# One attention and feed-forward layer: the closing output projection moved into the main block, with f16 operands

## The chip, the core and the metric

The kernel runs on one core of a Trainium2 chip. The core has five engines with instruction streams of their own: TensorE (PE, matrix products), VectorE (DVE), ScalarE (ACT), GpSimd (POOL) and SyncE (SP, which here only issues DMAs). They share the on-chip memory SBUF. Products land in PSUM, eight banks of 128 x 512 f32. Engines wait for one another by semaphores. The metric is the device time of one execution in microseconds; lower is better.

## What is computed

For x of 2048 tokens by 512 features, with xn the layer norm of x:

```
out  = x + attention(xn) @ Wo + bo + ffn(xn)
attention: 16 heads of 32, 4 key/value heads, causal, ALiBi bias
ffn: (gelu(xn @ Wg.T) * (xn @ Wu.T)) @ Wd.T, 4096 wide; Wg, Wu, Wd are unpacked from 4-bit codes and scales
```

The kernel keeps f32 accuracy by splitting operands into a rounded high part and a low part and adding three products (high x high, high x low, low x high).

## The kernel before

`preamble` normalises x, projects q, k and v into DRAM (`q_parts`, `k_parts`, `v_parts`) and computes scales, among them `oscale`, a scale for each output column that the `down` sums lack.

`main_loop` is a second block: 16 bodies, one for each attention head and, beside it, one sixteenth of the feed-forward width. A body has 48 slots, written out by hand in tables; every engine walks the same slots in program order. In a slot TensorE computes one block of scores (`score`, L1140, into the single bank `score_ps`), one or two products for the row maxima (`maximum`, L1118, into the two banks `pair_ps`, that is `max_ps` and `turn_ps`, in turn), half a piece of `gate` or `up` or a `down` tile (`mlp`, L1106 and L1086), and at some slots a batch of `values` (L1149). ScalarE turns a block of scores into exponentials (L1238), then into f16 (`phi`, L1245). TensorE's next score waits until the exponential has read the bank. GpSimd takes the low parts (`plo`, L1415). VectorE reduces maxima (L1342, L1338), adds `down` tiles to `acc` (`accumulate`, L1289), does the gelu products and, from slot 26 on, decodes the next weights (`decode_step`); TensorE turns these (L345), and ScalarE and VectorE copy them to `wh` (L352) and `wl` (L357).

A head's output leaves by another way (`output_steps`): ScalarE copies it out of PSUM (L1257, L1260), SyncE gathers it in SBUF (`gather_o`, three parts) and sends the row sums to `l_parts` in DRAM. In the next body SyncE loads the sums (`load_sums`), VectorE adds and inverts them (`row_sums`, slot 14), SyncE stores and spreads the reciprocals (`store_recips`, `spread_recips`), and GpSimd adds the parts (slots 19 and 23) and multiplies (`normalise`, slot 36). SyncE stores the result as f32 in `o_heads`.

`epilogue` is a third block. Every engine enters it after SyncE has left the second. It loads Wo, all heads' outputs and x, brings the last head through the same steps, splits Wo and the outputs into high and low parts (L1508, L1514, L1522), multiplies (`project`, L1531), turns `oscale` into a row by a product with ones, multiplies `acc` by it (L1587), adds x and the bias (L1591, L1566), adds the product (L1596) and stores 16 tiles.

## Time and profile before

| what | value |
|---|---|
| median of 3 runs | 1768.53 us (1766.18 to 1768.92) |
| profiled execution, own time | 1768.29 us |
| its span, first to last instruction | 1766.5 us |
| TensorE busy | 1677.6 us (95%) |
| VectorE, ScalarE, GpSimd busy | 1339.7, 1074.1, 963.7 us |

The profile lists, for one execution, when each instruction ran and what an engine waited for before it (in square brackets: the idle time, and who ended it). The numbers below count from the span's start. A timeline merges neighbours of the same kind (x4). The chain of waits is followed back from the last instruction to whatever released each step.

### The profile page before, as it was taken

How to read it: one execution, taken by the hardware profiler on the slowest of the kernel's cores; microseconds unless marked ns; L12 is line 12 of the kernel's file. 1: busy time of each engine (PE TensorE's matmuls, PEld its weight loads, DVE VectorE, ACT ScalarE, POOL GpSimd, SP SyncE). 2: the span in 40 equal slices, each digit the busy share in tenths (PEclk: the TensorE clock that was granted, in tenths of full speed). 3: DMA queues.
4: the chain of work that ended last, by engine and by line, in shares of the span. 5: the costliest groups of instructions: out<-in, count | busy, mean ns of one | idle time of the engine just before them, and what ended most of it. 6: DMA issues, size and time to landing. Idle time of an engine off the chain costs nothing. (4 is left out here: it accounts for less than half of the span.)

```text
span 1766.5 us, 30945 instructions
## 1 busy us (share of the span) xinstructions
PE 1677.6 (95%) x10368; PEld 854.4 (48%) x10368; DVE 1339.7 (76%) x2785; ACT 1074.1 (61%) x1779; POOL 963.7 (55%) x801
## 2 busy tenths in 40 slices
PE   4989999999999999999999999999999999999957
PEld 3764444444444444444444444444444444444435
DVE  6767778777777777787777777777777777777739
ACT  2336757575756667575857576766758575757610
POOL 3306647374655556473746565664737464656617
PEclk9999999999999999999999999999999999999979
DMA  6770020212020211202020202012030212020154
GB/s 192 201 192 18 20 69 17 74 26 75 26 69 18 70 29 30 70 17 76 24 74 27 70 21 78 16 42 59 17 81 20 74 26 74 21 73 17 46 176 155
DMA packets 94825, 109.49 MB, mean 62 GB/s; under 512 B 39068, under 2 KB 58524, under 8 KB 92876
## 3 DMA queue, kind: packets, MB, share of 16 engines
q1 hardware_dynamic: 94668, 107.53, 22.4%
q8 instruction: 83, 1.36, 0.3%
q14 instruction: 74, 0.61, 0.1%
HBM read 72.22 MB, written 22.41 MB: 54 GB/s over the span
## 5 line engine op out<-in xcount | busy, mean ns | idle before, releaser
L1415 POOL TENSOR_TENSOR plo<-p,phi 128x512 f16<-128x512 f32 (+1 forms) x576 | 669.8, 1174 | 317.8 <-ACT phi L1245 316.1
L1238 ACT ACTIVATE p<-score_ps,pshift 128x512 f32<-128x512 f32 (+1 forms) x576 | 382.2, 663 | 284.3 <-DVE score_ps L1327 155.7
L1245 ACT ACTIVATE phi<-p 128x512 f16<-128x512 f32 (+1 forms) x576 | 350.0, 608 | 15.3
L1423 POOL TENSOR_TENSOR il<-prod,ih 128x512 f16<-128x512 f32 x128 | 160.9, 1257 | 335.5 <-DVE ih L1321 335.5
L1140 PE MATMUL score_ps<-qst,kst 128*128 128x512 f32 (+3 forms) x640 | 305.6, 494 | 13.0 <-ACT p L1238 11.4
L1289 DVE TENSOR_TENSOR acc<-down_ps,acc 128x512 f32<-128x512 f32 x253 | 172.7, 682 | 70.0 <-PE down_ps L1086 70.0
L1342 DVE TENSOR_REDUCE mxp<-max_ps 128x1 f32<-128x512 f32 x256 | 175.5, 686 | 53.5 <-PE max_ps L1118 53.5
L1106 PE MATMUL gate_ps<-xh,wh 128*128 128x512 f16 x512 | 198.7, 388 | 0.0
L1106 PE MATMUL up_ps<-xh,wh 128*128 128x512 f16 x512 | 198.0, 387 | 0.0
L1086 PE MATMUL down_ps<-wh,ih 128*128 128x512 f16 x506 | 195.9, 387 | 0.9 <-DVE acc L1289 0.9
L1106 PE MATMUL gate_ps<-xh,wl 128*128 128x512 f16 x512 | 194.8, 380 | 0.0
L1106 PE MATMUL gate_ps<-xl,wh 128*128 128x512 f16 x512 | 194.7, 380 | 0.0
L1106 PE MATMUL up_ps<-xh,wl 128*128 128x512 f16 x512 | 194.0, 379 | 0.0
L1106 PE MATMUL up_ps<-xl,wh 128*128 128x512 f16 x512 | 194.0, 379 | 0.0
L1086 PE MATMUL down_ps<-wl,ih 128*128 128x512 f16 x506 | 191.8, 379 | 0.0
L1086 PE MATMUL down_ps<-wh,il 128*128 128x512 f16 x506 | 191.8, 379 | 0.0
L1140 PEld LDWEIGHTS score_ps<-qst,kst 128*128 128x128 f32 x640 | 116.3, 189 | 111.5 <-ACT p L1238 48.4
L1149 PE MATMUL o_ps<-phi,vst 128*32 128x512 f16 (+3 forms) x1744 | 164.4, 348 | 0.0
L1118 PE MATMUL max_ps<-kst,qst 128*128 128x512 f32 (+2 forms) x320 | 151.4, 473 | 10.3 <-SPq L1007 4.8
L1118 PE MATMUL turn_ps<-kst,qst 128*128 128x512 f32 (+3 forms) x320 | 141.2, 441 | 1.6 <-DVE mxp L1338 1.6
L1149 PE MATMUL o_ps<-plo,vst 128*32 128x512 f16 (+3 forms) x1024 | 136.2, 342 | 0.0
L1222 ACT ACTIVATE gl<-gate_ps,cur 128x512 f32<-128x512 f32 x128 | 87.8, 686 | 67.9 <-issue 42.6
(201 smaller groups left out, 2919.2 us busy)
## 6 DMA issues: line engine op xcount, KB each, us to landing
qst<-q_parts SPq DMA_DIRECT2D x204, 64.0 KB
kst<-k_parts SPq DMA_DIRECT2D x48, 256.0 KB, 6.1
o<-oraw SPq DMA_DIRECT2D x192, 64.0 KB
vst<-v_parts SPq DMA_DIRECT2D x16, 512.0 KB, 5.9
q_parts<-o SPq DMA_DIRECT2D x24, 256.0 KB, 3.3
raw<-L_ffn_gate_W_packed_dram SPq DMA_DIRECT2D x18, 256.0 KB, 2.8
raw<-n_L_ffn_up_W_packed_dram SPq DMA_DIRECT2D x18, 256.0 KB, 3.2
raw<-L_ffn_down_W_packed_dram SPq DMA_DIRECT2D x18, 256.0 KB, 3.9
```

What stands on the lines that cost most here:

```text
L1086: mm = nc.tensor.matmul(dst[:], lhs, rhs, start=(q == 0), stop=(q == 5))
L1106: mm = nc.tensor.matmul(dst[:], lhs, rhs, start=(q == 0), stop=(q == 11))
L1118: mm = nc.tensor.matmul(dst[:, 0:cols], qst[:, c, t * P:(t + 1) * P], kst[par][:, m * CH:m * CH + cols], start=True, stop=True)
L1140: mm = nc.tensor.matmul(score_ps[:, col:col + width], kst[par][:, j * P:(j + 1) * P], qst[:, c, tok:CH], start=True, stop=True, skip_group ...
L1149: mm = nc.tensor.matmul(bank[g * HD:(g + 1) * HD, tok:CH], vst[:, j, of * HD:(of + 1) * HD], src[n % PP][:, col:col + CH - tok], start=sta ...
L1222: nc.scalar.activation(gl[a][:], gate_ps[:], ACT.Square, scale=cur[par][:, a:a + 1]).then_inc(square_done, 1)
L1238: nc.scalar.activation(p32[n % PR][:, 0:cols], score_ps[:, 0:cols], ACT.Exp, bias=pshift[:, 0:1]).then_inc(exp_done, 1)
L1245: nc.scalar.activation(phi[n % PP][:, 0:cols], p32[n % PR][:, 0:cols], ACT.Copy).then_inc(phi_done, 1)
L1289: nc.vector.tensor_tensor(acc[:, n % NT, :], bank[:], acc[:, n % NT, :], ALU.add).then_inc(acc_done, 1)
L1342: nc.vector.tensor_reduce(mxp[c % 2][:, t, m:m + 1], pair_ps[n % 2][:, 0:cols], AX.X, ALU.max).then_inc(red_done, 1)
L1415: nc.gpsimd.tensor_tensor(plo[n % PP][:, 0:cols], p32[n % PR][:, 0:cols], phi[n % PP][:, 0:cols], ALU.subtract).then_inc(plo_done, 1)
L1423: nc.gpsimd.tensor_tensor(il[w % 2][:, a, :], prod[a][:], ih[w % 2][:, a, :], ALU.subtract).then_inc(il_done, 1)
```

## The change

The third block is gone; its work stands at the end of the second block's programs.

- Outputs of heads are stored as two f16 halves: `output_hi` on ScalarE at slot 38 and `output_lo` on GpSimd at slot 39 of the next body. The copies out of PSUM lose their scale operand; the scale goes into `yback`.
- Column scales and their inverses are turned into rows in the preamble (a transposition of 8 rows, a copy, a DMA). The `down` sums start from the bias times the inverse (`bias_row`), so `acc` is no longer cleared. VectorE, no longer GpSimd, writes the four constants at the start of the block.
- In the last body nothing is decoded or loaded for a next head. Wo is loaded at its start; VectorE looks for its largest element at slots 17 to 20 (eight reductions), scales at slot 29, and ScalarE and VectorE make its f16 halves at slots 31 to 35. The outputs of earlier heads are loaded for the first two of four blocks of 512 tokens.
- Behind the loop TensorE does the first three of four groups for eight tiles before, between and behind the last `down` tiles; the last group, which holds the last head, follows. ScalarE issues part of the loads, the bulk ones of blocks 2 and 3 late.
- In `gather_o` the row sums go first, in two DMAs and not four, with semaphores of their own; the reciprocals are spread by one DMA and not four.

```
-ADD_PARTS_AT, NORMALISE_AT = (19, 23), 36
+ADD_PARTS_AT, NORMALISE_AT, BIAS_AT = (19, 23), 36, 11
+OUTPUT_HI_AT, OUTPUT_LO_AT = 38, 39
+WO_MAX_AT, WO_SCALE_AT, WO_HI_AT = (17, 18, 19, 20), 29, (31, 32, 33, 34)
...
+        nc.gpsimd.tensor_tensor(o[:, 0, :], o[:, 0, :], o[:, step + 1, :], ALU.add).then_inc(osum_done, 1)
...
+    def output_hi(act, h):
+        act.wait_ge(on_done, h + 1)
+        if h:
+            act.wait_ge(on_out, 32 * h)
+        nc.scalar.activation(onh[:], o3[h % 2][:, 0, :], ACT.Copy).then_inc(ohi_done, 1)
+
+    def output_lo(pool, h):
+        pool.wait_ge(ohi_done, h + 1)
+        if h:
+            pool.wait_ge(on_out, 32 * h)
+        nc.gpsimd.tensor_tensor(onl[:], o3[h % 2][:, 0, :], onh[:], ALU.subtract).then_inc(olo_done, 1)
...
+                        pe.wait_ge(os_done, 1)
+                        pe.wait_ge(xl_done, KT * NCH)
+                        nc.tensor.transpose(turn[0][0:2 * KT, 0:P], oboth, ident[:]).then_inc(os_turned, 1)
...
                     load_v(i)
-                    load_k(nxt, 1 - par)
+                    if i < LAST:
+                        load_k(nxt, 1 - par)
+                    else:
+                        load_early()
+                    if i == 0:
+                        sp.wait_ge(os_out, 16)
+                        for row, src in ((column_inv, os_s[1]), (bias, bo)):
...
+                        if i == LAST and c == NCH - 2:
+                            spread_tops()
+                        if i == LAST and c == NCH - 1:
+                            sp.wait_ge(wo_lo, KVH)
+                            load_x(sp, 0)
...
-                    for m in range(3):
-                        sp.wait_ge(wf_done, (i + 1) * 6 + 2 * m + 2)
-                        load_raw(sp, m, (i + 2) % HEADS)
+                    if i + 2 < HEADS:
+                        for m in range(3):
+                            sp.wait_ge(wf_done, (i + 1) * 6 + 2 * m + 2)
+                            load_raw(sp, m, i + 2)
...
                 def gather_o(i, c, par):
                     sp.wait_ge(oraw_done, after(2 * (i * NCH + c + 1)))
                     if c == 0 and i >= 2:
-                        sp.wait_ge(on_done, i - 1)
+                        sp.wait_ge(ohi_done, i - 1)
+                        sp.wait_ge(olo_done, i - 1)
+                    if c == 0 and i == 1:
+                        sp.wait_ge(acc_done, after(NT))
+                    cols = slice(c * CH, (c + 1) * CH)
+                    sp.dma_start(l_s[par, 0:1, cols], oraw[c % 2][VPARTS * HD:VPARTS * HD + 1, :]
+                                 ).then_inc(l_out[c % 2], 16)
+                    sp.dma_start(l_s[par, 1:LPARTS, cols], lraw[0:(LPARTS - 1) * HD:HD, :]
+                                 ).then_inc(l_out[c % 2], 16)
                     for part in range(VPARTS):
                         sp.dma_start(o3[par][c * HD:(c + 1) * HD, part, :],
                                      oraw[c % 2][part * HD:(part + 1) * HD, :]).then_inc(o_out[c % 2], 16)
-                    cols = slice(c * CH, (c + 1) * CH)
-                    sp.dma_start(l_s[par, 0:1, cols], oraw[c % 2][VPARTS * HD:VPARTS * HD + 1, :]
-                                 ).then_inc(o_out[c % 2], 16)
-                    for q in range(1, LPARTS):
...
+                def load_early():
+
+                    sp.wait_ge(wf_done, 6 * HEADS)
+                    sp.wait_ge(wturn_done, 6 * HEADS)
+                    for g in range(KVH):
+                        sp.dma_start(wo[g], Wo.rearrange("(r g d) n -> g r d n", r=REP, g=KVH)[g]).then_inc(wo_in, 16)
...
+                    sp.wait_ge(on_out, 32 * (HEADS - REP))
+                    load_full(sp, 0)
...
+                    sp.wait_ge(wtop_done, 1)
+                    sp.dma_start(w_s.rearrange("(p o) -> p o", o=1), wtop).then_inc(wtop_out, 16)
+                    sp.wait_ge(wtop_out, 16)
+                    sp.dma_start(wall, w_s.rearrange("(o n) -> o n", o=1).broadcast_to([P, P])).then_inc(wall_in, 16)
+                    sp.wait_ge(down_done, after(LAST * ND))
+                    load_full(sp, 1)
...
+                load_sums(sp, LAST)
+                store_recips(sp, LAST)
+                spread_recips(sp, LAST)
+                sp.wait_ge(olo_done, HEADS)
+                load_last(sp, 1, onl)
+                for n in range(NT):
+                    sp.wait_ge(y_read, n + 1)
+                    sp.dma_start(out_d[n * P:(n + 1) * P, :], acc[:, n, :]).then_inc(out_done, 16)
...
-                        if s in TURN_W_AT:
+                        if s in TURN_W_AT and i < LAST:
...
+                def project(n, groups):
+
+                    c, t = n // TPC, n % TPC
+                    for g in groups:
+                        for q, (part, rhs) in enumerate(((0, woh), (0, wol), (1, woh))):
+                            mm = nc.tensor.matmul(y_ps[n % len(y_ps)][:], out_part(part, c, g)[:, t * P:(t + 1) * P],
+                                                  rhs[:, g, :], start=(g == 0 and q == 0), stop=(g == KVH - 1 and q == 2))
+                    if KVH - 1 in groups:
+                        mm.then_inc(y_done, 1)
+
                 loop(pe, body)
+                first, last = range(KVH - 1), range(KVH - 1, KVH)
+                pe.wait_ge(wo_lo, KVH)
+                pe.wait_ge(o_in[0], 16 * FULL_DMAS[0])
+                pe.wait_ge(red_done, after(HEADS * NMAX))
+                for n in range(2):
+                    project(n, first)
                 pe.wait_ge(gelu_done, after(HEADS * GU))
                 pe.wait_ge(prod_done, after(HEADS * GU))
                 pe.wait_ge(exp_done, after(HEADS * NBLK))
                 for t in range(TPC):
                     for half in range(2):
                         down(HEADS * NCH - 1, t, half, (down_ps, gate_ps, up_ps, score_ps)[t])
+                pe.wait_ge(oraw_done, after(2 * HEADS * NCH))
+                for n in range(2, TPC):
+                    project(n, first)
+                pe.wait_ge(o_in[1], 16 * FULL_DMAS[1])
+                for t in range(TPC):
+                    pe.wait_ge(acc_done, after((HEADS * NCH - 1) * TPC + t + 1))
+                    project(TPC + t, first)
+                for n in range(NT):
+                    if n % TPC == 0:
+                        pe.wait_ge(o_in[n // TPC], 16 * (FULL_DMAS[n // TPC] + 2))
+                        pe.wait_ge(last_in[n // TPC], 32)
+                    if n >= len(y_ps):
+                        pe.wait_ge(y_read, n - len(y_ps) + 1)
+                    project(n, last if n < len(y_ps) else range(KVH))
 
             @block.scalar
             def _(act):
@@ -1253,10 +1410,11 @@
                         done = BATCH_OF[BLK_END[c] - 1] + 1
...
                 loop(act, body)
+                act.wait_ge(on_out, 32 * LAST)
+                for c in range(2):
+                    load_rest(act, c)
+                act.wait_ge(il_done, after(HEADS * GU))
+                load_x(act, 1)
+                act.wait_ge(up_done, HEADS * GU)
+                load_full(act, 2)
+                load_rest(act, 2)
+                output_hi(act, LAST)
+                act.wait_ge(ohi_done, HEADS)
+                load_last(act, 0, onh)
+                load_full(act, 3)
+                load_rest(act, 3)
+                for c in range(2, NCH):
+                    load_x(act, c)
 
...
-                    nc.vector.tensor_tensor(acc[:, n % NT, :], bank[:], acc[:, n % NT, :], ALU.add).then_inc(acc_done, 1)
+                    before = acc[:, n % NT, :] if n >= NT else bias_row
+                    nc.vector.tensor_tensor(acc[:, n % NT, :], bank[:], before, ALU.add).then_inc(acc_done, 1)
...
+                        if i == LAST and s in WO_MAX_AT:
+                            wo_max(WO_MAX_AT.index(s))
+                        if i == LAST and s == WO_SCALE_AT:
+                            wo_scale()
+                        if i == LAST and s - 1 in WO_HI_AT:
+                            wo_low(WO_HI_AT.index(s - 1))
+                        if i == LAST:
+                            continue
...
+                    nc.vector.tensor_reduce(wmost[:, g:g + 1], wo[g], AX.X, ALU.max).then_inc(wmax_done, 1)
+                    nc.vector.tensor_reduce(wleast[:, g:g + 1], wo[g], AX.X, ALU.min).then_inc(wmax_done, 1)
...
+                def scale_sums(c):
+                    part = acc[:, c * TPC:(c + 1) * TPC, :]
+                    dve.wait_ge(acc_done, after((HEADS - 1) * NT + (c + 1) * TPC))
+                    if c == 0:
+                        dve.wait_ge(column_in, 16)
+                    nc.vector.tensor_tensor(part, part, column.unsqueeze(1).broadcast_to([P, TPC, C]), ALU.mult
+                                            ).then_inc(scaled, 1)
+
+                def add_x(c):
+                    dve.wait_ge(scaled, c + 1)
+                    dve.wait_ge(x_back[c], 16 * len(xr[c]))
+                    tiles = TPC // len(xr[c])
+                    for k, x in enumerate(xr[c]):
+                        part = acc[:, c * TPC + k * tiles:c * TPC + (k + 1) * tiles, :]
+                        last = nc.vector.tensor_tensor(part, part, x, ALU.add)
+                    last.then_inc(base_done, 1)
+
+                nc.vector.memset(pshift[:], PSHIFT).then_inc(pshift_done, 1)
+                nc.vector.memset(mask_row[:, 0:CH - P], 0.0).then_inc(mask_done, 1)
+                nc.vector.tensor_copy(mask_row[:, CH - P:], mask_ts[:]).then_inc(mask_done, 1)
+                nc.vector.tensor_scalar(identr[:], ident[:], 1.0, 1.0, ALU.mult, ALU.mult).then_inc(identr_done, 1)
                 dve.wait_ge(mask_done, 2)
                 loop(dve, body)
+                scale_sums(0)
...
                 loop(dve, body)
+                scale_sums(0)
+                add_x(0)
                 for t in range(TPC):
+                    if t == 2:
+                        row_sums(dve, LAST)
                     accumulate((HEADS * NCH - 1) * TPC + t, (down_ps, gate_ps, up_ps, score_ps)[t])
+                for c in range(1, NCH):
+                    scale_sums(c)
+                add_x(1)
+                for n in range(NT):
+                    if n >= 2 * TPC and n % TPC == 0:
+                        add_x(n // TPC)
+                    dve.wait_ge(y_done, n + 1)
+                    dve.wait_ge(base_done, n // TPC + 1)
+                    nc.vector.scalar_tensor_tensor(acc[:, n, :], y_ps[n % len(y_ps)][:], yback, acc[:, n, :],
+                                                   ALU.mult, ALU.add).then_inc(y_read, 1)
...
-                nc.gpsimd.memset(mask_row[:, 0:CH - P], 0.0).then_inc(mask_done, 1)
-                nc.gpsimd.tensor_copy(mask_row[:, CH - P:], mask_ts[:]).then_inc(mask_done, 1)
-                nc.gpsimd.tensor_scalar(identr[:], ident[:], 1.0, 1.0, ALU.mult, ALU.mult).then_inc(identr_done, 1)
-                nc.gpsimd.memset(pshift[:], PSHIFT).then_inc(pshift_done, 1)
-
-                nc.gpsimd.memset(acc[:], 0.0).then_inc(acc_done, 1)
...
+                        if i == 0 and s == BIAS_AT:
+                            pool.wait_ge(bias_in, 32)
+                            nc.gpsimd.tensor_tensor(bias_row, bias, column_inv, ALU.mult).then_inc(acc_done, 1)
...
+                        if i and s == OUTPUT_LO_AT:
+                            output_lo(pool, i - 1)
```

How the instructions stand, at three places. First TensorE, at the end of the loop. Before, the last half tile of the loop (`ih0`, `il0`) is followed by the last `down` tiles:

```order
L1086 MATMUL down_ps<-wh1,ih0 128x512
L1086 MATMUL down_ps<-wl1,ih0 128x512
L1086 MATMUL down_ps<-wh1,il0 128x512
L1086 MATMUL down_ps<-wh1,ih1 128x512
L1086 MATMUL down_ps<-wl1,ih1 128x512
L1086 MATMUL down_ps<-wh1,il1 128x512
```

Now (`turn_ps` and `max_ps` are output banks 0 and 1, `kst0` holds loaded outputs, `wl0` and `wh0` the high and low half of Wo):

```order
L1213 MATMUL down_ps<-wh1,ih0 128x512
L1213 MATMUL down_ps<-wl1,ih0 128x512
L1213 MATMUL down_ps<-wh1,il0 128x512
L1337 MATMUL turn_ps<-wl0,kst0 128x512
L1337 MATMUL turn_ps<-wh0,kst0 128x512
L1337 MATMUL turn_ps<-wl0,kst0 128x512 x2
```

Eighteen products with Wo, nine for each bank, stand ahead of the `down` tiles. Second, ScalarE in slots 38 and 39 of a body, before:

```order
L1238 ACTIVATE p32_2<-score_ps,pshift 128x512
L352 ACTIVATE wh1<-turn_ps 128x512
L1245 ACTIVATE phi5<-p32_2 128x512
L1228 ACTIVATE gl0<-gl0,cur0 128x512
L1238 ACTIVATE p32_0<-score_ps,pshift 128x512
```

Now (`o3_1` holds the last head's output, `onh` its f16 half):

```order
L1395 ACTIVATE p32_2<-score_ps,pshift 128x512
L285 ACTIVATE onh<-o3_1 128x512
L354 ACTIVATE wh1<-turn_ps 128x512
L1402 ACTIVATE phi5<-p32_2 128x512
L1385 ACTIVATE gl0<-gl0,cur0 128x512
L1395 ACTIVATE p32_0<-score_ps,pshift 128x512
```

The copy stands between the exponential of slot 38 and the weights' copy. Third, VectorE in slots 17 and 18 of the last body, before:

```order
L1321 CAST ih1<-prod0 128x512
L1342 TENSOR_REDUCE mxp1<-max_ps 128x1
L1289 TENSOR_TENSOR acc<-down_ps,acc 128x512
L1342 TENSOR_REDUCE mxp1<-turn_ps 128x1
L1342 TENSOR_REDUCE mxp1<-max_ps 128x1
```

Now (`wf` holds half of Wo, `sc0` the extremes found):

```order
L1505 CAST ih1<-prod0 128x512
L1526 TENSOR_REDUCE mxp1<-max_ps 128x1
L1592 TENSOR_REDUCE sc0<-wf 128x1
L1593 TENSOR_REDUCE sc0<-wf 128x1
L1473 TENSOR_TENSOR acc<-down_ps,acc 128x512
L1526 TENSOR_REDUCE mxp1<-turn_ps 128x1
L1592 TENSOR_REDUCE sc0<-wf 128x1
L1593 TENSOR_REDUCE sc0<-wf 128x1
L1526 TENSOR_REDUCE mxp1<-max_ps 128x1
```

Two reductions stand behind the maximum in front of the accumulation, and two behind the next one.

## Rows read from the trace of the kernel before

**Rows 1.** Waits chain that ended last: start us, duration us, what.
```profile
1688.89 11.29 DMA lp<-l_parts
...
1700.78 2.56 DMA l_recips<-lrec
...
1704.65 1.99 DMA rb<-l_recips
```
**Rows 2.** Windows: stretch, length, busy us (count) by engine, clock, DMA, GB/s.
```profile
160.00:1574.00 1414.00, 1400.21 (x8935) 677.23 (x8935) 1094.67 (x2318) 938.93 (x1558) 814.93 (x690) 1.00 0.17 45
...
1682.00:1766.50 84.50, 52.47 (x200) 41.57 (x200) 51.20 (x37) 9.77 (x6) 39.62 (x9) 0.81 0.51 168
```
**Rows 3.** Timeline of TensorE, slots 45 to 47: start us, us, instruction.
```profile
1669.33 0.38 PE L1106 MATMUL up_ps<-xh,wh 128*128 128x512 f16 x1
...
1671.70 0.38 PE L1106 MATMUL up_ps<-xl,wh 128*128 128x512 f16 x1
...
1675.05 0.38 PE L1086 MATMUL down_ps<-wh,il 128*128 128x512 f16 x1
```
**Rows 4.** Timeline of TensorE, closing block, its first idle stretch.
```profile
1726.79 0.50 PE L1531 MATMUL y_ps<-woh,och 128*128 128x512 f32 x1 [2.13 <-DVE xr L1596]
...
1728.16 0.63 PE L1531 MATMUL y_ps<-woh,ocl 128*128 128x512 f32 x1
1728.58 0.63 PE L1531 MATMUL y_ps<-woh,och 128*128 128x512 f32 x1
```
**Rows 5.** Timeline of VectorE, closing block.
```profile
1714.88 2.29 DVE L1587 TENSOR_TENSOR acc<-acc,orow 128x2048 f32<-128x2048 f32 x1
...
1732.62 6.52 DVE L1591 TENSOR_TENSOR acc<-acc,xr 128x2048 f32<-128x2048 f32 x1
...
1761.32 2.49 DVE L1596 TENSOR_TENSOR xr<-y_ps,acc 128x512 f32<-128x512 f32 x4
```
**Rows 6.** Timeline of GpSimd, closing block.
```profile
1730.40 6.59 POOL L1508 TENSOR_TENSOR ocl<-xl,och 128x2048 fp32r<-128x2048 f32 x1
```
**Rows 7.** Timeline of SyncE, last head's gather.
```profile
1675.93 2.94 SPq L1042 DMA_DIRECT2D o<-oraw  x3
```
**Rows 8.** Timeline of ScalarE, head 15, slots 38 and 39.
```profile
1654.84 0.70 ACT L1238 ACTIVATE p<-score_ps,pshift 128x512 f32<-128x512 f32 x1
...
1655.89 0.66 ACT L1245 ACTIVATE phi<-p 128x512 f16<-128x512 f32 x1
1656.41 0.75 ACT L1228 ACTIVATE gl<-gl,cur 128x512 f32<-128x512 f32 x1
1657.03 0.71 ACT L1238 ACTIVATE p<-score_ps,pshift 128x512 f32<-128x512 f32 x1
```
**Rows 9.** Timeline of TensorE, head 15, slot 40.
```profile
1657.79 0.49 PE L1140 MATMUL score_ps<-qst,kst 128*128 128x512 f32 x1 [0.30 <-ACT p L1238]
```
**Rows 10.** Waits of TensorE, 300:1575: total us, times, longest.
```profile
PE score_ps L1140 <- ACT p L1238: 8.5, 28, 0.3
```
**Rows 11.** Timeline of GpSimd, head 15, slot 36.
```profile
1653.98 1.46 POOL L279 TENSOR_TENSOR on<-on,rb 128x512 f32<-128x512 f32 x1
```
**Rows 12.** Timeline of VectorE, head 15, slots 19 to 21.
```profile
1617.91 0.69 DVE L1342 TENSOR_REDUCE mxp<-max_ps 128x1 f32<-128x512 f32 x1 [0.64 <-PE max_ps L1118]
...
1621.28 0.69 DVE L1289 TENSOR_TENSOR acc<-down_ps,acc 128x512 f32<-128x512 f32 x1 [2.08 <-PE down_ps L1086]
```
**Rows 13.** Timeline of TensorE, head 15, one turn of weights and what follows.
```profile
1665.34 0.60 PE L345 MATMUL turn_ps<-ident,wf 128*128 128x128 f32 x4
1665.69 0.48 PE L1140 MATMUL score_ps<-qst,kst 128*128 128x384 f32 x2
```
**Rows 14.** Timeline of ScalarE, then TensorE, start of the main block.
```profile
130.46 0.69 ACT L1222 ACTIVATE gl<-gate_ps,cur 128x512 f32<-128x512 f32 x1 [11.78 <-POOL pshift L1406]
...
132.19 0.38 PE L1118 MATMUL turn_ps<-kst,qst 128*128 128x256 f32 x1 [1.38 <-DVE mxp L1338]
```
**Rows 15.** Timeline of SyncE, head 15: spreading of the reciprocals.
```profile
1642.79 1.69 SPq L261 DMA_DIRECT2D rb<-l_recips  x4
```

382 lines of the change are left out of this document (170 added, 212 removed).

## The prediction

> **What bounds the kernel now.** Read first the windows by stage [rows 2]. From 160 to 1574 us TensorE is busy 1400.21 of 1414 us at full clock: the heads are bound by TensorE, and whatever the other engines do there is free unless TensorE waits for it. From 1682 us to the end, 84.5 us, no engine is full (TensorE 52, VectorE 51, GpSimd 40) and the granted clock is 0.81: this closing stretch is bound by a chain of hand-overs. The chain that ended last [rows 1] shows its head: the 32 KB load of the row sums takes 11.29 us, since it was issued behind the bulk loads, then 2.56 us to store the reciprocals and 1.99 us to spread them. Its second half is VectorE: an addition of 2048 columns takes 6.52 us [rows 5], where the multiplication of the same size beside an idle GpSimd takes 2.29 us. GpSimd's operation began at 1730.40 and ended at 1736.99 [rows 6], and VectorE's ended 2.15 us after that: it had stood still until GpSimd was through.
>
> **The closing stretch.** The last work of TensorE inside the head loop starts at 1675.05 [rows 3]. Twelve f16 matmuls of 512 columns start between 1669.33 and 1671.70, so one follows another after 2.37 / 11 = 0.2155 us; loop work ends at 1675.27, and from there to the end of the span are 91.2 us. In the new order TensorE has 216 such matmuls left: 24 `down` and 16 tiles of 12 (three products over four groups instead of the same number in 4-byte form). Three quarters of eight tiles, 72 matmuls, need nothing of the last head, and stand before, between and behind the `down`s. I take TensorE as nearly continuous: 216 x 0.2155 = 46.5, plus 0.02 for each of 24 starts of a piece, 0.5, plus 0.2 because the last matmul runs 0.38 rather than 0.22, plus 0.7 for VectorE's last operation (a pitch of 2.49 / 4 in [rows 5], and its start), plus 2.7 for the last store (VectorE's four last operations end at 1763.81, the span at 1766.5). That is 50.6 us.
>
> Does the last head arrive in time? TensorE starts its last-group products after 24 + 72 matmuls plus starts, at 1675.3 + 20.8 = 1696.1. The chain: the gather begins at 1675.93 [rows 7] and now sends the sums first, so they land at about 1679 and the load of the sums, with nothing of its own queue ahead, at about 1681 (2 us, as the spreading took [rows 1]). VectorE takes the row sums between its second and third accumulation. It first multiplies 2048 columns (2.29), adds x (the same size, 2.3) and waits for the second `down`: sums and reciprocals are done at 1683.2. Store 2.56 gives 1685.8; spreading, with its issue, 2.4 gives 1688.2. Now GpSimd must multiply, and VectorE is in three multiplications of 2.29 us that read two operands from SBUF. By rows 5 and 6 these two engines exclude each other. VectorE's second one ends at 1689.8, GpSimd's 1.4 us (1.46 in [rows 11]) at 1691.2, ScalarE's copy 0.6 later; VectorE has taken its third until 1693.5, GpSimd's subtraction of 1.3 ends at 1694.8, and its first load lands 2 us later, 1696.8. TensorE waits 0.7 us. Stretch after: 51.3, **saved 39.9**.
>
> The Trainium skill, SBUF — State Buffer (SBUF: two separate sides), says that the port pair shared by VectorE and GpSimd is an exclusive lock held for a whole instruction. By the reverse case alone, GpSimd never blocked, the chain would end at about 1693.4 and the wait would be nothing; by the page it is the 0.7 us above. The chain's slack is used up either way, so a later link is paid in full.
>
> **The heads.** The new copy to f16 (`output_hi`) stands on ScalarE in slot 38, between the exponential and two copies. There ScalarE has no gap: operations start at 1654.84, 1655.89, 1656.41 and 1657.03 [rows 8], and the exponential of slot 39 ends at 1657.74; TensorE's score of slot 40, which needs its bank, starts at 1657.79 after waiting [rows 9]. This recurs: 28 such waits from 300 to 1575 us, at most 0.3 each [rows 10], one or two a head. A copy from SBUF costs 0.52 (1655.89 to 1656.41) and lands wholly on that wait. It also waits for GpSimd's normalisation, which ends at 1655.44 [rows 11], 0.03 after ScalarE would be there. Against it stands 0.07, an estimate: the copies out of PSUM lose their scale operand (0.70 with such an operand, 0.66 without in [rows 8]; two of them close ahead). Net 0.45. Behind the copy are queued the weights' copy, the probabilities' copy and the exponential. Heads 1 to 14 pay it, 14 x 0.45 = **6.3 lost**; head 15 has no weights to copy there. GpSimd's subtraction (about 1.3) comes before the probabilities of slot 39, which TensorE needs only two slots later: nothing. On SyncE one spreading DMA replaces four and two row-sum DMAs four, while one more store of outputs is added; no engine of a head waits for them: nothing. The same holds for moving the sums ahead of the outputs in each gather.
>
> **Head 15.** It no longer turns next weights: six turns of 1665.69 - 1665.34 = 0.35 [rows 13], 2.1 saved. VectorE gets eight reductions in slots 17 to 20, about 0.6 each (as the four operations of [rows 5] are spaced), and two small ones: 5.2. Its idle time there is 0.64 + 2.08 = 2.7 at least [rows 12]; the rest, 2.5, meets TensorE, which runs only two maxima ahead of it. I take 1.5 lost. Queued behind are the maxima and the accumulation. The scale search and the four low parts come where decoding was: nothing. **Saved 0.6**; between 2.7 saved (hidden) and 3 lost.
>
> **The start.** ScalarE waited until 130.46 for a constant that GpSimd wrote late [rows 14], and TensorE then 1.38 us for the maxima behind it. VectorE now writes it at once; GpSimd's clearing of the sums is gone. I take 2.2 saved, TensorE's wait and a part of what follows. The turned column scales add a small transposition, a copy and a DMA before the block's hand-over, about 0.7. **Saved 1.5**, between 0.5 lost and 3.5 saved.
>
> **Sum.** 39.9 - 6.3 + 0.6 + 1.5 = 35.7. The profiled execution took 1768.29 for a span of 1766.5, and the median of three runs is 0.24 above it: 1768.29 - 35.7 + 0.24 = 1732.8, **1733 us**.
>
> **Rivals.**
> *The copy is hidden.* If ScalarE catches up before slot 40 or TensorE's later waits shrink, the heads cost 0 to 2 and the time is 1727 to 1729. For it: the wait is only 0.3, and ScalarE is idle a third of each head. Against: between slots 38 and 40 it has no gap.
> *The chain ends later.* ScalarE now issues 12 bulk and part loads right after the loop, while the sums travel. The 11.29 us [rows 1] show what bulk ahead does in one queue. If the sums take 4 us more, TensorE stands 5 us; after 2.13 us idle [rows 4] it soon ran at a pitch of 0.42, the lower level (1.2 GHz), for about eight matmuls, 1.7 us. Time 1737 to 1740. The Trainium skill, DMA: Bandwidth & Descriptors (Issuing engines are not separate DMA queues), supports this: DMAs started by different engines run on the same 16 DMA engines and interleave.
> *Dearer heads.* The copy waits for the normalisation and for its own issue, 1.0 a head, or the search costs 4: 1740 to 1744.
> *Slower than before.* The one place: ScalarE now stands in order behind the normalisation, and so behind the spread reciprocals. If these land late, exponentials stop in each head. It decides at 35.7 + 6.3 = 42 us over 15 heads, 2.8 us a head: 1769 to 1780. Against: the spreading is issued at 1642.79 [rows 15], 11 us before its use [rows 11], and lands in 2.
> *The change doesn't bite:* some wait keeps the 72 early matmuls behind the last head. They are 15.5 us: about 1748.
>
> **Chances.** Forecast (1729 to 1737) 0.50; hidden copy 0.22; later chain 0.17; dearer heads 0.06; early matmuls held 0.03; slower 0.02. The range 1725 to 1742 holds the first three and half the fourth. About 0.2% (3.5 us) is what a measurement can tell from no change; faster 0.97, same 0.01, slower 0.02.
>
> **What would show it.** After the loop TensorE should run with one gap under 1 us at about 1696, at full clock, to about 1722 plus the heads' shift. The load of the sums should take 2 to 3 us, not 11. In each head the score of slot 40 should wait about 0.8 us on the exponential. In head 15 TensorE should wait for the maxima of slots 18 to 20, 1 to 2 us. At the start ScalarE's first square should come about 2 us earlier. I am wrong if TensorE idles over 3 us after the loop, if the time from one head to the next doesn't grow, or if it grows by over 1 us.

## The result, and where the time went

| what | before | after |
|---|---|---|
| median | 1768.19 us (1766.18 to 1768.92, 4 runs) | 1737.18 us (1736.2 to 1738.53, 4 runs) |
| ratio, 95% interval | | 0.9826 (0.9814 to 0.9838) |
| profiled span | 1766.5 us | 1736.2 us |

The forecast was 1733, the range 1725 to 1742. The time lies in the range, 4 us above the forecast and at the lower edge of the rival "the chain ends later" (1737 to 1740). So the gain is real (31 us), but one part of the reasoning was off, and one of my own signs of being wrong came true: TensorE idled over 3 us after the loop. The page of the kernel after, its span and its first section:

```profile
span 1736.2 us, 30755 instructions
PE 1666.9 (96%) x10337; PEld 830.9 (48%) x10337; DVE 1312.1 (76%) x2782; ACT 1067.0 (61%) x1788; POOL 935.9 (54%) x807
```

These rows of TensorE's timeline cut the span into the stretches of my sum (start, length, engine, line, operation, and the idle time before it). They are the first maximum of the main block, the scores of slot 40 of heads 0, 1 and 14, and the first product of the output projection, with which the loop's work ends:

```profile
123.62 0.45 PE L1245 MATMUL max_ps<-kst,qst 128*128 128x128 f32 x1 [5.51 <-SPq L1099]
...
203.56 0.50 PE L1267 MATMUL score_ps<-qst,kst 128*128 128x512 f32 x1 [0.29 <-ACT p L1395]
...
300.88 0.50 PE L1267 MATMUL score_ps<-qst,kst 128*128 128x512 f32 x1 [0.82 <-ACT p L1395]
...
1566.61 0.50 PE L1267 MATMUL score_ps<-qst,kst 128*128 128x512 f32 x1 [0.82 <-ACT p L1395]
...
1680.95 0.38 PE L1337 MATMUL turn_ps<-wl,kst 128*128 128x512 f16 x1
```

| stretch | before | after | change | predicted |
|---|---|---|---|---|
| up to TensorE's first maximum of the main block | 122.46 | 123.62 | +1.2 | +0.7 |
| from there to slot 40 of head 0 | 82.33 | 79.94 | -2.4 | -2.2 |
| 14 heads, slot 40 to slot 40 | 1356.13 | 1363.05 | +6.9 | +6.3 |
| slot 40 of head 14 to the end of the loop | 114.35 | 114.34 | 0.0 | -0.6 |
| from there to the end of the span | 91.2 | 55.25 | -36.0 | -39.9 |
| sum | 1766.5 | 1736.2 | -30.3 | -35.7 |

Of the 5.4 us that are missing in the profiled execution, 3.9 are in the closing stretch. TensorE's timeline at its one wait there:

```profile
1705.42 0.58 PE L1337 MATMUL turn_ps<-wl,kst 128*128 128x512 f16 x1 [3.59 <-DMA kst<-onl]
1705.80 0.63 PE L1337 MATMUL turn_ps<-wh,kst 128*128 128x512 f16 x1
...
1708.64 0.38 PE L1337 MATMUL o_ps<-wl,kst 128*128 128x512 f16 x1
```

The load of the last head's low part (`load_last`) came 3.59 us late, not 0.7. The matmuls behind it then start 0.43 us apart instead of 0.2155: eight intervals take 3.22 us where they should take 1.72, so another 1.5 us is lost at TensorE's lower level (1.2 GHz; the granted clock of 1702 to 1709 us is 0.76, that of the stretches beside it 1.00). A row of windows has the start and end, the length, busy time and count of each engine, the granted clock, the mean busy share of the DMA engines, and GB/s:

```profile
core 0: us, PE busy (x) PEld busy (x) DVE busy (x) ACT busy (x) POOL busy (x), PEclk, DMA share, GB/s
1681.00:1702.00 21.00, 20.83 (x97) 9.26 (x95) 18.08 (x17) 1.13 (x3) 4.33 (x4) 1.00 0.46 141
1702.00:1709.00 7.00, 3.58 (x10) 1.36 (x11) 1.80 (x3) 0.00 (x0) 1.31 (x1) 0.76 0.54 169
1709.00:1736.00 27.00, 23.98 (x112) 10.64 (x109) 14.54 (x16) 0.00 (x0) 0.00 (x0) 1.00 0.64 236
```

The chain that brings this load, from the timelines of SyncE, VectorE and GpSimd:

```profile
1684.54 0.52 SPq L242 DMA_DIRECT2D lp<-l_parts  x1
1690.90 0.35 SPq L256 DMA_DIRECT2D l_recips<-lrec  x1
1694.32 0.62 SPq L263 DMA_DIRECT2D rb<-l_recips  x1
```

```profile
1690.32 0.26 DVE L247 TENSOR_REDUCE lsum<-lp 128x16 f32<-128x64 f32 x1 [2.01 <-DMA lp<-l_parts]
```

```profile
1699.47 1.68 POOL L279 TENSOR_TENSOR o<-o,rb 128x512 f32<-128x512 f32 x1 [10.09 <-DMA rb<-l_recips]
```

Three small transfers stand between these rows: the load of the row sums took 5.8 us (1684.54 to 1690.32), the store of the reciprocals 3.4 (1690.90 to 1694.32), their spreading 5.15 (1694.32 to 1699.47). I had put 2, 2.6 and 2.4. Two causes offered themselves: ScalarE's bulk loads in flight beside them, and VectorE's three multiplications of 2048 columns, which run until 1698.8 and might have held GpSimd. The experiments start there.

### The profile page after: what moved, and what is told of

It reads as the page before. It is cut to its first block, busy times and chain, and to the rows that moved or that the text cites. A ratio compares the mean times of both kernels' runs of the same rounds, so it can differ in the third digit from the quotient of the medians.

```text
span 1736.2 us, 30755 instructions
## 1 busy us (share of the span) xinstructions
PE 1666.9 (96%) x10337; PEld 830.9 (48%) x10337; DVE 1312.1 (76%) x2782; ACT 1067.0 (61%) x1788; POOL 935.9 (54%) x807
## 4 chain that ended last, share of the span: by engine, by line
PE 74%; DVE 8%; issue 6%; ACT 5%; DMA 0%; POOL 0%; SPq 0%; POOLq 0%; DVEq 0%; ACTq 0%
PE up_ps L1233 16%; PE down_ps L1213 16%; PE gate_ps L1233 15%; PE o_ps L1276 8%; PE score_ps L1267 8%; PE max_ps L1245 4%; PE turn_ps L1245 3%; ACT p L1395 2%; DVE mxp L1526 2%; PE l_ps L1276 2%; ACT wh L354 1%; PE max_ps L347 1%; DVE score_ps L1511 1%; DVE gl L1482 1%; DVE acc L1473 1%
## 5 line engine op out<-in xcount | busy, mean ns | idle before, releaser
L1668 POOL TENSOR_TENSOR plo<-p,phi 128x512 f16<-128x512 f32 (+1 forms) x576 | 661.0, 1158 | 317.6 <-ACT phi L1402 316.3
L1473 DVE TENSOR_TENSOR acc<-down_ps,acc 128x512 f32<-128x512 f32 x237 | 161.8, 683 | 62.4 <-PE down_ps L1213 62.1
```

The costliest lines, as they stand in the source:

```text
L1473: nc.vector.tensor_tensor(acc[:, n % NT, :], bank[:], before, ALU.add).then_inc(acc_done, 1)
L1668: nc.gpsimd.tensor_tensor(plo[n % PP][:, 0:cols], p32[n % PR][:, 0:cols], phi[n % PP][:, 0:cols], ALU.subtract).then_inc(plo_done, 1)
```

## Experiments

All ratios are to the kernel before, run on the same chip. "Last head 15" is the time from slot 40 of head 14 to the end of the loop; "closing" is the time from there to the start of TensorE's last matmul, which leaves out the last stores.

| kernel | median us | ratio (95%) | last head 15 | closing |
|---|---|---|---|---|
| after | 1737.18 | 0.9826 (0.9814 to 0.9838) | 114.34 | 51.65 |
| e1_bulk_late | 1736.76 | 0.9828 (0.9813 to 0.9843) | 114.34 | 51.62 |
| e2_port_free | 1734.05 | 0.9809 (0.9795 to 0.9824) | 114.34 | 49.31 |
| e3_bulk_and_port | 1739.52 | 0.9839 (0.9824 to 0.9853) | 114.32 | 54.37 |
| e4_copy_41 | 1726.00 | 0.9763 (0.9747 to 0.9779) | 113.95 | 51.07 |
| e5_wo_high | 1728.17 | 0.9770 (0.9755 to 0.9784) | 114.20 | 50.60 |
| e6_wo_search | 1731.88 | 0.9787 (0.9772 to 0.9802) | 117.71 | 51.21 |
| e7_bulk_behind_spread | 1726.42 | 0.9757 (0.9743 to 0.9772) | 114.00 | 48.76 |
| e8_spread_and_port | 1725.13 | 0.9747 (0.9731 to 0.9764) | 113.96 | 46.40 |
| e9_spread_in_four | 1723.93 | 0.9747 (0.9732 to 0.9761) | 113.95 | 46.41 |
| e10_wo_high_early | 1732.61 | 0.9800 (0.9783 to 0.9816) | 119.88 | 47.58 |
| e11_constants_back | 1731.98 | 0.9793 (0.9778 to 0.9807) | 113.98 | 51.31 |
| e12_best | 1722.20 | 0.9737 (0.9724 to 0.9750) | 113.37 | 46.41 |

Runs e5 to e12 stand on e4 (the copy in slot 41); e9 and e10 stand on e8 too, and e12 on e9. The kernel before had medians of 1767.3 to 1769.3 in these sessions, so kernels of different sessions are compared by ratio, or by the stretches of their profiles.

### e1: bulk loads behind the load of the sums

```
                 act.wait_ge(on_out, 32 * LAST)
+                act.wait_ge(e["lp_in"], 16 * HEADS)
                 for c in range(2):
                     load_rest(act, c)
```

> ScalarE waits for the row sums' load to land (16 x 16 signals) before it issues its ten bulk and part loads. In the changed kernel that 32 KB load took 5.8 us (issued at 1684.54, used at 1690.32), where its median over the heads is 1.9 us. Theory A, shared transfers: the bulk loads in flight make it slow. Then it takes 2 to 3 us here, VectorE's row sums come about 3 us earlier, and all behind them; TensorE's wait of 3.59 us for the last head's part shrinks to about 0.5 us, and the seven matmuls at a pitch of 0.43 us behind it run at 0.22. Time 1732.5 to 1734. Rival B, the sums are slow by themselves (a read just behind its own write): the load still takes over 5 us, nothing moves, 1737, or later since the bulk now lands later. Rival C, GpSimd's normalisation is held by VectorE alone (port): the load is quick but the normalisation starts at the same distance behind VectorE's third multiplication; as these multiplications stand behind the row sums on VectorE they move with them, so the gain is 1 to 2 us at most: 1735 to 1736.

Nothing was won. SyncE's timeline, then GpSimd's:

```profile
1682.56 0.52 SPq L242 DMA_DIRECT2D lp<-l_parts  x1
1686.82 0.35 SPq L256 DMA_DIRECT2D l_recips<-lrec  x1
1690.22 0.62 SPq L263 DMA_DIRECT2D rb<-l_recips  x1
```

```profile
1698.17 1.27 POOL L279 TENSOR_TENSOR o<-o,rb 128x512 f32<-128x512 f32 x1 [11.24 <-DMA rb<-l_recips]
```

Theory A is right for its own link: the sums had landed by 1684.67, when ScalarE, which waits for them, issued its first load. That is 2.1 us, where it was 5.8. The bulk then ran beside the next links: the store still took 3.4 us, the spreading 7.95 (1690.22 to 1698.17) instead of 5.15. All that was won was given back. The mean busy share of the DMA engines was about 1.0 from 1690.2 to 1694 here, while the spreading was in flight; in the kernel after it was 0.98 during the load of the sums (1686 to 1690) and 0.14 during the spreading. What I had not thought of is that a chain has three small transfers, and bulk that is moved off the first meets the third.

### e2: VectorE's multiplications behind GpSimd

```
                 for c in range(1, NCH):
+                    if c == 2:
+                        dve.wait_ge(olo_done, HEADS)
                     scale_sums(c)
```

> VectorE multiplies the third and fourth quarter of the sums by the column scales only once GpSimd's subtraction (the last head's low part) is done; the second quarter is multiplied before. In the changed kernel the three multiplications ran from 1692.13 to 1698.82 and GpSimd's normalisation started at 1699.47, while the spreading of the reciprocals was issued at 1694.32. Theory C, shared port: the reciprocals had landed at about 1696.5 and GpSimd stood behind VectorE; here the normalisation starts at about 1696.5, TensorE's wait shrinks from 3.59 to about 0.7 us. If the final additions, now behind the two late multiplications, don't hold TensorE's banks, the time is 1733 to 1734.5. Rival: the reciprocals land only at 1699.4, the normalisation starts there as before, and the two multiplications behind it come on top for VectorE: TensorE waits for a bank before its ninth tile, 1738 to 1741.

VectorE's and GpSimd's timelines:

```profile
1689.27 2.28 DVE L1626 TENSOR_TENSOR acc<-acc,raw 128x2048 f32<-128x2048 f32 x1
1700.50 4.49 DVE L1626 TENSOR_TENSOR acc<-acc,raw 128x2048 f32<-128x2048 f32 x2 [8.95 <-POOL onl L291]
```

```profile
1697.31 1.27 POOL L279 TENSOR_TENSOR o<-o,rb 128x512 f32<-128x512 f32 x1 [9.56 <-DMA rb<-l_recips]
```

VectorE is idle from 1691.55, and still GpSimd starts only at 1697.31, 4.86 us after the spreading was issued (1692.45). So theory C falls: GpSimd waited for the reciprocals, not for VectorE. The run is nevertheless 2.3 us better in its closing stretch. By its rows the reciprocals landed 17.9 us after the loop's end instead of 18.5, GpSimd's two operations took 1.27 and 1.16 us instead of 1.68 and 1.42, and TensorE's wait was 2.17 us, behind which it stayed at its upper level. The feared bank wait is there, 0.41 us before the ninth tile. Not all of the gain belongs to the edit, which doesn't touch the load of the sums: that load took 4.4 us here and 5.8 in the kernel after, and between 4.0 and 6.8 in e4, e5, e6 and e11, whose code behind the loop is that of the kernel after. With that same code TensorE's wait ranges from 2.35 to 3.59 us, and the intervals of e2 and of the kernel after overlap. What the edit alone is worth stays open here; the reading on theory C doesn't hang on it.

### e3: both

> Both edits: ScalarE's bulk loads behind the row sums' load, and VectorE's last two multiplications behind GpSimd's subtraction. If transfers and port each hold the chain and add up, the chain ends 6 us earlier, before TensorE wants it (it is ready at 1701.8): no wait in the closing stretch, full clock, 1731.5 to 1733. If only one of the two holds the chain, the time is that of the better of the two alone. If VectorE becomes the bound (ninth tile waits for the first final addition), a wait of 1 to 3 us appears about 5.2 us after the last head's part, and the time is 1733 to 1736.

```profile
1707.30 0.58 PE L1337 MATMUL turn_ps<-wl,kst 128*128 128x512 f16 x1 [5.25 <-DMA kst<-onl]
```

None of the three cases that I had written down. The spreading, issued at 1692.38, landed at 1702.15: 9.8 us, while VectorE did nothing. This is what suggested that the spreading itself had become the long link and that the bulk was what stretched it; e7 and e8, without bulk, bear it out (5.2 us).

### e4: the f16 copy in slot 41

```
-OUTPUT_HI_AT, OUTPUT_LO_AT = 38, 39
+OUTPUT_HI_AT, OUTPUT_LO_AT = 41, 42
```

> The copy of the outputs to f16 moves from slot 38 to slot 41 of ScalarE, the subtraction from 39 to 42 of GpSimd. In the changed kernel a head takes 97.33 us against 96.87, and the score of slot 40 waits 0.82 us instead of 0.30. Theory: the copy's 0.5 us is paid because ScalarE has no gap between slots 38 and 40; in slot 41 ScalarE idles 2.57 us before the exponential and 0.97 us before the next. The head falls back to 96.87 us, 14 heads give back 6.9 us: 1730 to 1731. Rival: the head is longer for another reason (GpSimd's 1.4 us subtraction between its operations, SyncE's two stores more): the wait in slot 40 or a new one stays, 97.2 to 97.4 us a head, 1736 to 1738.

ScalarE's timeline in head 14 (the copy is L285), and TensorE's score of slot 40 in head 1:

```profile
1561.71 0.69 ACT L1395 ACTIVATE p<-score_ps,pshift 128x512 f32<-128x512 f32 x1 [2.57 <-PE score_ps L1267]
1562.30 0.62 ACT L285 ACTIVATE onh<-o 128x512 f16<-128x512 f32 x1
...
1564.03 0.69 ACT L1395 ACTIVATE p<-score_ps,pshift 128x512 f32<-128x512 f32 x1 [0.59 <-DVE score_ps L1511]
```

```profile
298.40 0.50 PE L1267 MATMUL score_ps<-qst,kst 128*128 128x512 f32 x1 [0.29 <-ACT p L1395]
```

The same copy costs nothing three slots later. The wait of slot 40 is back at 0.29 us, and from head 1 to head 14 a head takes (1557.25 - 298.40) / 13 = 96.83 us, where it took 97.36 (from 300.88 to 1566.61) and 96.87 in the kernel before. That is 7.4 us over 14 heads. The run was faster than expected (1730 to 1731): its profile has 0.4 us less in head 15 (there too the copy had stood in slot 38, and the score of slot 40 had waited 0.43 us) and 0.6 us less in the closing stretch besides, and the rest lies ahead of head 0, where profiles scatter (below).

### e5, e6, e10, e12: Wo's search, scale and high parts in head 15

The tables alone change in e5, e6 and e10 (in e12 two high parts stand in slot 28):

```
 e4   WO_MAX_AT, WO_SCALE_AT, WO_HI_AT = (17, 18, 19, 20), 29, (31, 32, 33, 34)
 e5                                      (17, 18, 19, 20), 29, (31, 32, 36, 37)
 e6                                      (13, 17, 21, 25), 31, (32, 33, 36, 37)
 e10                                     (17, 18, 19, 20), 27, (27, 28, 30, 31)
 e12                                     (17, 18, 19, 20), 28, (28, 28, 30, 31)
```

Why they were run: in the kernel after, TensorE's place in head 15, compared piece by piece with the kernel before, falls back by 1.17 us in slots 17 to 20 (the search) and by 1.68 us in slots 34 to 36; the six turns left out, and the wait of slot 44 that is gone, give 2.85 us back. ScalarE's timeline ahead of the second loss, and TensorE's score of slot 34 behind it:

```profile
1650.23 0.68 ACT L1395 ACTIVATE p<-score_ps,pshift 128x512 f32<-128x512 f32 x1
1650.80 0.72 ACT L1448 ACTIVATE wl<-wf,sc 128x512 f16<-128x512 f32 x1
1651.41 0.63 ACT L1402 ACTIVATE phi<-p 128x512 f16<-128x512 f32 x1
1651.93 0.60 ACT L1415 ACTIVATE oraw<-o_ps 128x512 f32<-128x512 f32 x1
1652.41 0.59 ACT L1418 ACTIVATE lraw<-l_ps 96x512 f32<-96x512 f32 x1
1652.89 0.72 ACT L1385 ACTIVATE gl<-gl,cur 128x512 f32<-128x512 f32 x1
1653.50 0.68 ACT L1395 ACTIVATE p<-score_ps,pshift 128x512 f32<-128x512 f32 x1
```

```profile
1654.23 0.51 PE L1267 MATMUL score_ps<-qst,kst 128*128 128x512 f32 x1 [0.95 <-ACT p L1395]
```

There is no gap in these 3.9 us, and one of Wo's high parts (L1448) stands among them.

> On top of the copy in slot 41 (1726.0 us): Wo's four high parts on ScalarE in slots 31, 32, 36 and 37, where the weights' copies of an ordinary head stand, instead of 31 to 34; the low parts move with them. In head 15 TensorE fell back by 1.3 us at its score of slot 34 (1642.04 to 1644.89 where the kernel before took 1.54 us, a wait of 0.95 us on the exponential) and by 0.4 us in the two slots behind. Theory: slots 33 and 34 hold the copies of the outputs and sums out of PSUM, and two more copies of 0.57 us there queue the exponentials. Then both losses go: 1.3 to 1.7 us less, 1724.3 to 1724.7. Rival: ScalarE is full in slots 31 to 37 whichever two slots are taken, and slots 36 and 37 now queue the exponentials of slots 38 to 40: the wait moves there, 1725.5 to 1726.5.

```profile
1645.42 0.50 PE L1267 MATMUL score_ps<-qst,kst 128*128 128x512 f32 x1 [0.96 <-ACT p L1395]
1653.78 0.50 PE L1267 MATMUL score_ps<-qst,kst 128*128 128x512 f32 x1 [0.38 <-ACT p L1395]
```

The rival held: the wait of slot 34 is unchanged, since the high part of slot 32 is still ahead of it, and slot 39 has a new one. The high parts take the places of the weights' copies of an ordinary head, but TensorE's turns, which kept it back there, are gone. My reading is that TensorE is now ahead and waits for ScalarE, so that leaving out its turns saves little where ScalarE's copies stay; no run takes the turns out alone.

> On top of the copy in slot 41 (1726.0 us): the search for Wo's largest element in slots 13, 17, 21 and 25 of VectorE instead of 17 to 20, the scale in slot 31 instead of 29, the high parts in slots 32, 33, 36 and 37. The search put TensorE 1.17 us behind between slots 17 and 20 in head 15. Theory: VectorE's spare time between slots 13 and 25 covers one pair of reductions each four slots, and the 1.2 us go, and with the high parts moved most of the 1.7 us too: 1723.2 to 1724.5. Rival: VectorE's small gaps can't be collected, since TensorE runs only two maxima ahead; each pair costs 0.3 us wherever it is, and only the high parts' share is won: 1724.5 to 1725.2. A later scale could make ScalarE wait for it in slot 32: then over 1727.

Worse than every case but the last, which I had only mentioned: the last reduction now ends at 1627.1, the scale is ready at 1642.0, and VectorE stood 4.19 us for the spread maxima, then ScalarE for VectorE:

```profile
1640.87 0.29 DVE L1602 TENSOR_REDUCE sc<-sc 128x1 f32<-128x128 f32 x1 [4.19 <-DMA sc<-wo_tops]
```

TensorE's score of slot 34 then waited 2.41 us. The pairs in slots 13 and 25 cost too (TensorE waits of 0.90 and 0.75 us on the exponential behind them), so whether small gaps of VectorE could be collected elsewhere stays open.

> The run with bulk behind the spreading and the port kept free, and Wo's scale in slot 27 of VectorE, its high parts in slots 27, 28, 30 and 31 of ScalarE. With 31, 32, 36 and 37 the wait of 0.96 us in slot 34 stayed and another of 0.38 us came in slot 39. Theory: in slots 31 to 34 ScalarE has no gap (two copies out of PSUM, a gelu and an exponential each slot), so any copy there holds TensorE, and the turns of weights that head 15 leaves out save TensorE nothing as long as ScalarE's copies stay; ahead of slot 28 ScalarE idles 2.26 us. The wait in slot 34 falls to 0.4 us or less and the later ones go: head 15 is 1.2 to 1.8 us shorter from its slot 28 to the loop's end. From slot 40 of head 14 to the end of the loop: 112.2 to 112.8 us instead of 113.96. Rival: the scale in slot 27 comes before the spread maxima have landed, VectorE and then ScalarE stand, and TensorE waits for the row of maxima or a score in slots 27 to 28: 114 or more.

```profile
1634.41 0.72 ACT L1448 ACTIVATE wl<-wf,sc 128x512 f16<-128x512 f32 x1 [2.97 <-DVE sc L1614]
1635.04 0.57 ACT L1407 ACTIVATE qst<-score_ps 2x512 fp32r<-2x512 f32 x1
```

```profile
1635.66 0.79 PE L1267 MATMUL score_ps<-qst,kst 128*128 128x384 f32 x2 [3.71 <-ACT qst L1407]
```

The rival held, and dearly: behind the first high part stands the copy of the row of maxima (L1407), which the next scores need; TensorE waited 3.71 us and then lost 2.8 us in the next slot at the lower clock (the granted clock of 1636 to 1642 us is 0.53). Behind that point, though, TensorE won 0.6 us against e4.

> The run with the spreading in four loads (copy in slot 41, bulk behind the spreading, port kept free), and Wo's scale in slot 28 of VectorE, its high parts twice in slot 28 and once in 30 and 31 of ScalarE. With the scale and the first high part in slot 27, the row of maxima stood behind them on ScalarE and TensorE waited 3.71 us, with up to 2.8 us more at the lower clock behind it; from slot 28 on that run won back 0.7 us against the high parts in 31 to 34. Theory: in slot 28 the high parts stand behind the exponential and in front of 2.3 us in which ScalarE idles, and nobody waits for them. Then the 3.71 us and the clock's share are gone and the 0.7 us stay: from slot 40 of head 14 to the end of the loop 113.2 to 113.4 us instead of 113.96, ratio to before 0.9742 to 0.9747 where 0.9747 was had. Rival: the spread maxima have not landed when VectorE comes to the scale in slot 28 (in slot 27 it waited 1.06 us), ScalarE stands behind it, and the next exponential and TensorE wait up to 1 us: ratio 0.975 to 0.9755.

```profile
1644.37 0.49 PE L1268 MATMUL score_ps<-qst,kst 128*128 128x512 f32 x1 [0.67 <-ACT p L1396]
```

In slot 28 the two high parts cost nothing, and the wait of slot 34 is 0.67 us instead of 0.96: 113.37 us instead of 113.95 for this stretch. But a wait stays in slot 34 although no high part stands in slots 32 to 34: against the kernel before, TensorE still falls back by 1.0 us in slots 34 to 36 (1.7 in the kernel after). At 1722.20 us e12 has the lowest time of the study, by ratio (0.9737 against 0.9826) some 16 us better than the kernel after; against e9 (0.9747) the intervals overlap, and only the stretch tells the two apart.

### e7, e8, e9: the chain behind the loop

e7 makes ScalarE wait for the spread reciprocals (`rb_in`) before all bulk, puts two short loads, `output_hi` and `load_last` first, and adds x to the second quarter later; e8 adds the edit of e2 to it. e9 spreads in four loads:

```
-        sp.dma_start(rb[:], r_s[h % 2].rearrange("(c o t) -> c o t", o=1, t=CH).broadcast_to([NCH, HD, CH])
-                     ).then_inc(rb_in, 16)
+        for c in range(NCH):
+            sp.dma_start(rb[c * HD:(c + 1) * HD, :], r_s[h % 2, c * CH:(c + 1) * CH].rearrange("(o t) -> o t", o=1)
+                         .broadcast_to([HD, CH])).then_inc(rb_in, 16)
```

> On top of the copy in slot 41 (1726.0 us): ScalarE waits until the reciprocals are spread (load landed) before it issues any bulk load, takes the two short parts for the first half first, then the copy and the last head's store, then the rest; x is added to the second quarter only after the first quarter is finished. Holding the bulk until the sums' load alone gave a load of 2.1 us instead of 5.8, but a spreading of 7.9 us instead of 5.2 (1690.22 to 1698.17). Theory: the bulk slows whichever of the three small transfers it meets. With none in flight the load takes 2.1, the spreading 2 to 2.6 us, the normalisation starts 2 to 4 us earlier, TensorE's wait of 2.82 us (copy in slot 41) shrinks to under 0.5 us: 1723.3 to 1724.3. Rival 1: the spreading is slow by itself in the last head: wait and time stay. Rival 2: the bulk now lands too late for TensorE's ninth tile or for VectorE's additions of x: a new wait of 2 to 5 us, 1726 to 1729. Rival 3: VectorE's multiplications now hold GpSimd, since the reciprocals land inside them: up to 2.3 us of the gain is lost, 1724.5 to 1726.

SyncE's timeline, and GpSimd's:

```profile
1678.57 0.34 SPq L256 DMA_DIRECT2D l_recips<-lrec  x1
1679.99 0.62 SPq L263 DMA_DIRECT2D rb<-l_recips  x1
```

```profile
1685.22 3.18 POOL L279 TENSOR_TENSOR o<-o,rb 128x512 f32<-128x512 f32 x1 [6.55 <-DMA rb<-l_recips]
```

Three things at once. Without bulk the store takes 1.4 us, not 3.4. The spreading takes 5.2 us with no bulk beside it: rival 1 holds for this link. And now that the reciprocals land inside VectorE's third multiplication (the three run from 1680.59 to 1687.28, the last from about 1685.0), the normalisation takes 3.18 us and ends 1.1 us behind it: rival 3. TensorE waits 0.69 us for the last head, and 1.34 us for the third block's outputs, which come late (rival 2, in small).

> The run with the bulk behind the spreading, and VectorE's last two multiplications behind GpSimd's subtraction. If VectorE's multiplications hold GpSimd once the reciprocals land early, this one has the normalisation 1 to 2 us earlier than the run without it and is 0 to 1.5 us faster: 1722.8 to 1723.8. If they don't, it is the same or up to 1 us slower, as VectorE's final additions start later.

```profile
1688.90 1.27 POOL L279 TENSOR_TENSOR o<-o,rb 128x512 f32<-128x512 f32 x1 [6.50 <-DMA rb<-l_recips]
```

1.27 us for the same operation beside an idle VectorE: the port costs 1.9 us in e7. The ratio 0.9747 against e7's 0.9757 is within the intervals; the closing stretch, 46.40 against 48.76 us, shows it. No wait of TensorE's is left there. It is a near thing: e10 has the same code behind the loop, and there TensorE waited 1.00 us for the third block's outputs (closing stretch 47.58).

> The reciprocals are spread by four loads of 64 KB each, as in the kernel before, instead of one of 256 KB; the rest is the run with bulk behind the spreading and the port kept free. There the one load took 5.18 us (1683.73 to 1688.91) with nothing beside it; my prediction took 2.4, from the last of four smaller loads. Theory: the single load is slow by its form (one 64-partition-wide load each quarter ran in 2.0 us after its issue; four issues take 1.72 us). Then the reciprocals land 3.3 to 4 us after the first issue, 1.2 to 1.9 us earlier than with one; in the closing stretch TensorE no longer waits anyway (loop end to end of span 51.56 us), so the time stays within 0.5 us: ratio to before 0.974 to 0.9755. Rival: spreading takes 5 us in either form in the last head, being limited by 256 KB: no change in the normalisation's start either. In the heads neither shows.

```profile
1682.30 1.72 SPq L264 DMA_DIRECT2D rb<-l_recips  x4
```

```profile
1685.72 1.26 POOL L280 TENSOR_TENSOR o<-o,rb 128x512 f32<-128x512 f32 x1 [4.75 <-DMA rb<-l_recips]
```

Four loads of a quarter each are all there 3.4 us after the first issue; the one large load needs 5.2. The time stays the same, as expected, because nobody waits for it any more. The windows point to why the one load is slow. First e7, with the single load alone in flight, then e9:

```profile
1682.00:1684.00 2.00, 2.00 (x11) 0.92 (x10) 2.00 (x2) 0.00 (x0) 0.00 (x0) 1.00 0.26 98
```

```profile
1684.00:1685.00 1.00, 1.00 (x6) 0.49 (x5) 1.00 (x1) 0.00 (x0) 0.00 (x0) 1.00 0.54 137
```

The last two columns are the mean busy share of the 16 DMA engines and GB/s. The share is a quarter for the single load, and half in the busiest microsecond of the four. The Trainium skill, DMA: Bandwidth & Descriptors (Rules for kernel authors), says that an outermost dimension of fewer than 16 entries confines a DMA to at most that many engines; here it is 4, one for each block of tokens. By that rule the share would be 4 / 16 = 0.25, and the trace has 0.24 to 0.26 (e8 and e7). Which of the engines carried the bytes, no trace here tells.

### e11: the constants back on GpSimd

The four constants of the main block are written by GpSimd, as in the kernel before; `acc` is still not cleared.

> The copy in slot 41 (1726.0 us), and the main block's constants written by GpSimd again, in an order with the exponential's constant last, but without the clearing of the sums. From TensorE's first maximum of the main block to its score of slot 40 of head 0 it was 82.33 us in the kernel before and 79.4 to 80.2 in the kernels after the change. Theory: ScalarE's and TensorE's start waited for GpSimd, whose constants came only at 130.08, 7.3 us after its first two. Then this stretch is 81.5 to 82.3 again, and the time 1728 to 1728.5. Rival: the clearing of the sums (6.92 us on GpSimd, and VectorE's cast of 1.13 us beside it) was the cause: the stretch stays at 79.5 to 80.2, 1726.

GpSimd's timeline, then TensorE's:

```profile
128.43 0.29 POOL L1692 TENSOR_SCALAR identr<-ident 128x128 fp32r<-128x128 f32 x1 [8.00 <-issue]
```

```profile
130.53 0.39 PE L1245 MATMUL turn_ps<-kst,qst 128*128 128x256 f32 x1 [2.42 <-DVE mxp L1522]
```

From TensorE's first maximum to slot 40 of head 0 this run takes 83.98 us, e4 79.55, the kernel before 82.33. The theory held: with the constants back on GpSimd the gain is gone. But the stretch is also 1.65 us longer than in the kernel before, and the windows show where this comes from:

```profile
130.50:134.00 3.50, 3.46 (x11) 1.54 (x12) 2.29 (x5) 1.02 (x2) 0.00 (x0) 0.55 0.74 162
```

Behind the wait of 2.42 us (1.38 in the kernel before) the granted clock is 0.55; at the same place of e4 and of the kernel before it is 1.00. The next pieces of maxima take 5.39 us instead of 3.74. So this run overstates the constants by the price of the lower clock. And the clearing did have a part. VectorE's cast beside it, in the kernel before and here:

```profile
136.45 1.13 DVE L1321 CAST ih<-prod 128x512 f16<-128x512 f32 x1
```

```profile
136.44 0.43 DVE L1505 CAST ih<-prod 128x512 f16<-128x512 f32 x1
```

The cast is 0.70 us shorter without the clearing beside it, and TensorE's second score behind it waits 0.71 us on the exponential instead of 1.41, here as in the kernel after.

## Why the prediction was right or wrong

**The sum and its sign were right**: the last block's hand-overs and slow 4-byte products were worth 36 us of the profiled span (39.9 predicted), and the heads paid a part of it back. No run takes the hand-overs and the products apart, so their shares are argued and not shown.

**Closing stretch, 51.3 predicted, 55.25 measured.** The count of matmuls and their pitch were right: without a wait (e8, e9, e12) the last of them starts 46.4 us after the loop's end; I had 47.2 to its end, they give 46.8. TensorE was ready for the last head 20.9 us after the loop's end (20.8 predicted). What failed are two terms of the chain; times from the loop's end:

| step | predicted | after | e8 |
|---|---|---|---|
| sums and reciprocals done | 7.9 | 9.9 | 7.8 |
| spreading issued | 10.5 | 13.4 | 9.3 |
| reciprocals landed | 12.9 | 18.5 | 14.5 |
| normalisation done | 15.9 | 20.2 | 15.7 |
| TensorE starts on the last head | 21.5 | 24.5 | 20.7 |

First, I let the load of the sums run with "nothing of its own queue ahead", and so in 2 us. It shares the DMA engines with what ScalarE issues: 5.8 us, and 2.1 without (e1); the store 3.4, and 1.4 without (e7). This was the mechanism of the rival "the chain ends later" (0.17). I had priced its link and the clock right (4 us more for the sums, 1.7 for the clock), its wait of TensorE's too long (5 us against 3.59), and put the likelier case without it. The load and the store together put the spreading 2.9 us later than predicted. Second, the spreading: I took 1.99 us from [rows 1], which is the last of four loads from its issue, and added its issue; but the change replaces four loads by one of another shape, and that step I had waved through ("nothing"). It is 5.2 us without any neighbour, and in the kernel after it had none either: the busy share of the DMA engines during it is 0.14.

```profile
1694.30:1699.50 5.20, 5.20 (x25) 2.35 (x24) 5.20 (x5) 0.00 (x0) 0.03 (x1) 1.00 0.14 50
```

Against them stands what the port didn't cost: I had it hold GpSimd for 3.3 us in the sum, and in the kernel after the reciprocals land behind VectorE's last multiplication. The lock itself is as predicted, and e7 shows it: 3.18 us against 1.27. So two errors of about 3 us each were partly hidden by a third of almost the same size. That the time stayed in the range is in this part luck. The prediction also said that the chain's slack is used up with or without the lock; by its own numbers 2.7 us would be left without it (1693.4 against 1696.1). Behind a wait of 3.59 us the clock cost 1.5 us, as the rival had it (1.7).

**Heads.** Right in place, mechanism and size: 0.49 us a head against 0.45, the score of slot 40 waits 0.82 us on the exponential, as forecast. e4 takes the cost away and nothing else. The rival "the copy is hidden" fell, but only for slot 38.

**Head 15.** 0.0 instead of -0.6, for a reason that is not in my sum. The search cost 1.17 us (1.5 predicted). But the step named the four low parts on VectorE and not the four high parts on ScalarE, and TensorE fell back by 1.68 us in slots 34 to 36, where ScalarE has no gap. Moving the high parts away won 0.6 us of it (e12); the rest stays without them, by the reading in e5 because TensorE comes there too early. The copy in slot 38, which I had put at nothing for this head, cost 0.4 us (e4). Against these stand the turns and the wait of slot 44 left out: 2.85 us, with the copy already taken off, where I had 2.1. For the heads I had looked for ScalarE's gaps in slots 38 and 39 [rows 8]; I had not asked the same question of slots 31 to 34.

**Start.** -2.4 against -2.2, by ScalarE's first square and TensorE's waits, as forecast. By the rows of both kernels 1.65 us of it are the wait for the maxima (1.38 us) and what hangs on it, which e11 puts down to the constants, and 0.7 us are VectorE's cast, which the clearing had slowed. The 0.7 us for the transposition and its DMA can't be told: the main block starts at 123.62 here and between 119.0 and 124.3 in the twelve other profiles, in which nothing ahead of it differs from the kernel after.

## What to carry to other kernels

Before an operation is added to an engine in a loop, look up where that engine has a gap between two results that others wait for: the same 0.5 us copy cost 7 us in one slot and nothing three slots on. A chain of small transfers is slowed by bulk beside any of its links, though another engine issued the bulk (e1, e3); hold the bulk until the last link has landed, not the first. When several DMAs are merged into one, look at the outermost dimension of the new one: fewer instructions can mean fewer DMA engines.

## What the runs showed of the hardware that was not expected

- One 256 KB load with an outermost dimension of 4 took 5.2 us at a DMA share of 0.26; four of 64 KB, issued one after another, took 3.4 us at 0.54.
- Bulk loads issued by ScalarE stretched single transfers issued by SyncE: the load of the sums (32 KB) from 2.1 us (e1) to 5.8 in the kernel after and 4.0 to 6.8 in e2, e4, e5, e6 and e11; the store of the reciprocals from 1.4 (e7) to 3.4; and the spreading from 5.2 (e7) to 8.0 (e1) and 9.8 (e3).
- VectorE's cast of 512 columns took 1.13 us beside GpSimd's clearing of `acc` and 0.43 us without it.
- GpSimd's third instruction of the block began 8.0 us after its second (7.3 in the kernel before), with no wait that the profile shows. What it did in this time is open.
